# A two-layer attention kernel: head 1's score maxima over three PSUM banks, three of them ahead of the first score step, and two small VectorE operations rewritten as reductions

## The chip, the cores and the metric

The kernel runs on one core of a Trainium2 chip. The metric is device time in microseconds for one launch, which handles all eight images. TensorE does the matrix products and writes them to PSUM (eight banks of 512 fp32 numbers per partition); VectorE (DVE), ScalarE (ACT) and GpSimd (POOL) work on SBUF, the first two on PSUM as well. SyncE (SP) only issues DMAs. Each engine runs its own instructions in order and waits on semaphores for the others.

## The reference

Eight images of 32x32 positions with 384 channels. In short:

```
x = x + conv_attention(group_norm(x, 32 groups))     # 6 heads of 64, 1024 x 1024 scores,
                                                     # plus relative positions rel_h, rel_w
t = tokens(x)
t = t + causal_attention(layer_norm(t))              # 6 heads of 64, causal mask
t = t + gelu(layer_norm(t) @ kron(c_fc_1, c_fc_2).T) @ kron(c_proj_1, c_proj_2).T
attention: qkv = x @ W; softmax(q k^T * scale [+ rel]) v; @ W_out + bias
```

All products keep fp32 accuracy by splitting a number into an fp16 high part and an fp16 low part, and multiplying high x high, high x low and low x high.

## The kernel before, in words

**Order.** Everything is written out by hand, per engine: there is no scheduler. The closures `tensor`, `scalar`, `vector`, `gpsimd` and `sync` inside `build` (L1557 to L1784) issue one image after the other. While one image's feed-forward runs, TensorE already computes the next image's queries and keys between the `up` and `down` products (`after.fill`), then its relative positions (`rel_products`) and the first value tile (`v_products(pe, 0)`).

**An attention** (`class Attention`, L827) works through heads, and each head through G groups of two key tiles for half of the queries: 8 groups per head in the first attention, so 48 steps. A step `i` on TensorE (`tensor`, L1026) is: score products (`score_tiles`, six 128x512 products), one or two small "uses" (`early`), the weighted values of step i - 3 (`weighted_values`, 24 products), more uses (`late`). ScalarE turns scores into exponentials (L1073) and their fp16 high part (L1053); GpSimd, and VectorE in odd steps, make the low part (L1139). A ring of four buffers lies between.

**Maxima.** The softmax of a head subtracts the rows' maxima. For that, TensorE computes the scores another time in coarse form, 16 tiles of 128x512 per head (uses `("max", h, n)`, L941), VectorE takes each tile's maximum over 512 keys into `mxp` (L1097), `combine` (L1132) takes the larger of the two key halves, TensorE transposes the result to a row (use `("row", h)`, L946), VectorE copies it to `rowt` (L1105), and SyncE sends it to one row of `qc` by DMA (`row_in`), from where the last product of a score step (L992) adds it. Head 0's 16 tiles stand in the attention's `prologue`. Head 1's are spread over steps 0 to 4 (four, three, three, three, three), and its row is a late use of step 5. Head h's later tiles are spread in the same way ahead of its row.

**Banks.** Scores use banks 0 to 3 (two per step, in turn). The uses after the first row alternate between banks 4 and 5. Weighted values go to bank 6 for a head's first half and bank 7 for its second. A use waits until VectorE has released (`free`) the last use of its bank. Value tiles `v_products(pe, t)` go to banks 6 and 7 in turn; tile t waits for ScalarE's copies (`v_high`, L815 and L816, semaphore `v32`) of tile t - 2. `rel_high` (ScalarE, L740) and `rel_low` (VectorE, L746) copy the relative positions into the queries, 16 parts per image.

**The feed-forward's end.** VectorE's `low(i)` (`pair_low`, L614) makes the next image's key low parts, one instruction per head of pair i. `o2_out` (L1457) copies the `down` product out of PSUM, and TensorE's `spread` (L1465) waits for it. `eps` (L1264) adds epsilon to the variances, GpSimd's `root` (L1269) raises them to -1/2.

## Time and profile before

| what | value |
|---|---|
| median of 3 runs | 2788.88 us (2784.71 to 2790.33) |
| profiled execution | 2787.91 us, its span 2786.2 us |
| TensorE busy | 2597.0 us, 93% |
| ScalarE busy | 1996.5 us, 72% |
| VectorE busy | 1907.6 us, 68% |
| GpSimd busy | 1680.8 us, 60% |
| granted TensorE clock | 0.989 of full speed (mean) |
| chain of waits that ended last | TensorE 45%, GpSimd 17%, ScalarE 13%, VectorE 13%, issue 11% |

The profile is of one execution. Times in it are microseconds from the span's start. A row of a timeline has start, duration, engine, line, operation, and in brackets the idle time just before it with what ended it. Successive matmuls overlap in it by about 0.16 us, so the duration of a group of them is longer than the time after which the next one is issued. L numbers are lines of this kernel.

### The profile page before, as it was taken

To read this page: it belongs to the slowest core of one execution; us is meant where nothing else is said; L and a number is where in the kernel's file an instruction comes from. 1 tells how busy PE (TensorE), PEld (TensorE's weight loads), DVE (VectorE), ACT (ScalarE), POOL (GpSimd) and SP (SyncE) were. 2 spreads that over 40 slices of the span, in tenths; PEclk is the share of its full clock that TensorE was granted. 3 is DMA by queue.
4 is the path that set the end of the run, shared out by engine and by line. 5 is a ranking of instruction groups with operands and counts; after the bars stand their busy time and mean duration, and the time that the engine had idled before them with its cause. 6 is when DMAs were issued, how large, how long until landed. Compare 5 with 4: busy or idle time off the path is not lost.

```text
span 2786.2 us, 69295 instructions
## 1 busy us (share of the span) xinstructions
PE 2597.0 (93%) x29061; PEld 1540.1 (55%) x29061; DVE 1907.6 (68%) x3554; ACT 1996.5 (72%) x2387; POOL 1680.8 (60%) x1151
## 2 busy tenths in 40 slices
PE   7899999999999999999999999999998999999996
PEld 4465645656456564565645656466564655546563
DVE  8775757667676767757667576675776758677574
ACT  6686867858578595785867867678667777678684
POOL 5474756747567384683756747567465665747464
PEclk8999999999999999999999999999999999999998
DMA  3100012000110002000020000300003000110000
GB/s 110 40 2 2 2 33 72 2 1 2 48 57 2 1 2 76 28 2 1 2 84 21 2 1 2 103 2 2 1 8 97 2 2 2 24 58 2 2 2 24
DMA packets 52278, 64.50 MB, mean 23 GB/s; under 512 B 8672, under 2 KB 46176, under 8 KB 51968
## 3 DMA queue, kind: packets, MB, share of 16 engines
q1 hardware_dynamic: 50208, 59.66, 7.1%
q8 instruction: 231, 3.78, 0.6%
q10 hardware_dynamic: 1760, 0.41, 0.1%
q14 instruction: 79, 0.65, 0.1%
HBM read 30.75 MB, written 12.58 MB: 16 GB/s over the span
## 4 chain that ended last, share of the span: by engine, by line
PE 45%; POOL 17%; ACT 13%; DVE 13%; issue 11%; DMA 0%; SPq 0%; POOLq 0%; ACTq 0%; DVEq 0%
POOL pl L1139 16%; PE ps L571 9%; PE ps L1022 7%; PE ps L802 5%; PE ps L979 4%; PE ps L992 4%; PE ps L941 4%; ACT p L1073 4%; DVE mxp L1097 3%; PE ps L981 3%; ACT ph L1053 3%; DVE stats L1255 2%; DVE x L1251 2%; ACT qa L740 2%; PE ps L1230 2%
## 5 line engine op out<-in xcount | busy, mean ns | idle before, releaser
L1139 POOL TENSOR_TENSOR pl<-p,ph 128x1024 f16<-128x1024 f32 (+2 forms) x672 | 1095.9, 1644 | 366.8 <-ACT ph L1053 360.7
L1097 DVE TENSOR_REDUCE mxp<-ps 128x1 f32<-128x512 f32 (+2 forms) x1344 | 783.6, 626 | 265.4 <-PE ps L941 261.9
L1073 ACT ACTIVATE p<-ps 128x1024 f32<-128x1024 f32 (+1 forms) x672 | 640.3, 953 | 171.9 <-PE ps L992 171.1
L1053 ACT ACTIVATE ph<-p 128x1024 f16<-128x1024 f32 (+1 forms) x672 | 669.3, 996 | 21.4
L1022 PEld LDWEIGHTS ps<-v,ph 128*128 128x128 f16 x9600 | 506.2, 97 | 128.2 <-issue 27.5
L1022 PE MATMUL ps<-v,ph 128*128 128x65 f16 (+1 forms) x9600 | 531.1, 194 | 17.0 <-POOL pl L1139 16.5
L1022 PE MATMUL ps<-v,pl 128*128 128x65 f16 x4800 | 509.2, 192 | 0.0
L1022 PEld LDWEIGHTS ps<-v,pl 128*128 128x128 f16 x4800 | 446.7, 99 | 0.0
L992 PE MATMUL ps<-qc,kc 65*128 65x512 f16 (+3 forms) x1344 | 380.1, 364 | 0.0
L1139 DVE TENSOR_TENSOR pl<-p,ph 128x512 f16<-128x512 f32 (+1 forms) x336 | 243.9, 726 | 183.8 <-ACT ph L1053 182.8
L820 POOL TENSOR_TENSOR v<-o,v 128x384 f16<-128x384 f32 x128 | 115.7, 921 | 309.8 <-ACT o L816 309.3
L979 PE MATMUL ps<-qa,ka 128*128 128x512 f16 x768 | 291.1, 379 | 0.8 <-DVE qb L746 0.8
L981 PE MATMUL ps<-qb,ka 128*128 128x512 f16 x768 | 291.0, 379 | 0.0
L941 PE MATMUL ps<-ka,qa 128*128 128x512 f16 x768 | 256.1, 386 | 32.8 <-DVE mxp L1097 20.5
L992 PEld LDWEIGHTS ps<-qc,kc 65*128 65x128 f16 (+1 forms) x1344 | 123.5, 98 | 126.1 <-issue 1.9
L941 PEld LDWEIGHTS ps<-ka,qa 128*128 128x128 f16 x768 | 74.4, 97 | 170.1 <-DVE mxp L1097 67.2
L979 PE MATMUL ps<-qa,qb 128*128 128x512 f16 (+1 forms) x576 | 162.0, 344 | 2.1 <-ACT p L1073 2.1
L571 PE MATMUL ps<-xin,wqkv_hi 128*128 128x512 f16 x576 | 157.0, 381 | 2.2 <-DVE xin L521 2.2
L941 PE MATMUL ps<-qb,qa 128*128 128x512 f16 (+2 forms) x576 | 154.9, 326 | 0.0
L1126 DVE TENSOR_TENSOR lT<-ps,hT 128x512 f16<-128x512 f32 x96 | 66.4, 691 | 127.4 <-ACT hT L1058 127.4
L815 ACT ACTIVATE v<-ps 128x384 f16<-128x384 f32 x128 | 63.6, 497 | 118.2 <-PE ps L802 117.6
L1443 ACT ACTIVATE p<-ps 128x1024 f32<-128x1024 f32 x96 | 97.6, 1022 | 55.9 <-PE ps L1430 55.3
(197 smaller groups left out, 4664.1 us busy)
## 6 DMA issues: line engine op xcount, KB each, us to landing
xin<-in_x SPq DMA_DIRECT2D x8, 1536.0 KB, 6.8
x<-in_x SPq DMA_DIRECT2D x8, 1536.0 KB, 6.8
out<-x SPq DMA_DIRECT2D x16, 768.0 KB, 3.6
qc<-qa SPq DMA_DIRECT2D x42, 128.0 KB
qa<-qa SPq DMA_DIRECT2D x21, 128.0 KB
qb<-qb SPq DMA_DIRECT2D x21, 128.0 KB, 2.4
qa<-o SPq DMA_DIRECT2D x56, 48.0 KB
qb<-o SPq DMA_DIRECT2D x56, 48.0 KB, 2.0
```

Of the source, the lines that this page charges most:

```text
L571: mm = nc.tensor.matmul(m.ps[:, self.bank[i] + j, :], w[:, k, self.order[i] * P:(self.order[i] + 1) * P], x(k, 4 * j, 4 * j + 4), start=(n ...
L802: mm = nc.tensor.matmul(m.ps[:, 6 + t % 2, 0:C], flat_tile(x(k, t, t + 1)), w[:, k, 2 * C:3 * C], start=(n == 0), stop=(n == len(steps) - 1))
L820: self.nc.gpsimd.tensor_tensor(self.m.v[:, t, :, HD + 1:VW], self.m.o[:, t, :].rearrange("p (h d) -> p h d", d=HD), self.m.v[:, t, :, 0:HD ...
L941: mm = nc.tensor.matmul(m.ps[:, bank, 0:w], m.qa[:, sl, qt * P:(qt + 1) * P], self.ka[:, sl, kh * BANK:kh * BANK + w], start=not diag, sto ...
L979: nc.tensor.matmul(outs[j], self.ka[:, sl, keys[j]], m.qa[:, sl, q], start=True, stop=False)
L981: nc.tensor.matmul(outs[j], self.ka[:, sl, keys[j]], m.qb[:, sl, q], start=False, stop=False)
L992: mm = nc.tensor.matmul(outs[j], m.kc[crows(h), sl, keys[j]], m.qc[crows(h), sl, q], start=False, stop=True)
L1022: mm = nc.tensor.matmul(m.ps[:, 6 + half % 2, c0:c0 + w], e, v, start=(first and n == 0), stop=(g in self.last_of_half and n == len(work) ...
L1053: self.nc.scalar.activation(m.ph[:, i % RING, :, 0:w], m.p32[:, i % RING, :, 0:w], ACT.Copy).then_inc(self.s["hi"], 1)
L1073: nc.scalar.activation(m.p32[:, i % RING, :, 0:w], m.ps[:, 2 * (i % 2):2 * (i % 2) + 2, 0:w], ACT.Exp, scale=SCALE).then_inc(s["exp"], 1)
L1097: nc.vector.reduce_max(m.mxp[:, h % 2, kh, qt:qt + 1], m.ps[:, bank, 0:w], AX.X).then_inc(s["free"], 1)
L1139: engine.tensor_tensor(m.pl[:, i % RING, part, 0:w], m.p32[:, i % RING, part, 0:w], m.ph[:, i % RING, part, 0:w], ALU.subtract).then_inc(s ...
```

## The change

Seven edits, in one file:

1. The combine is a reduction over the two key halves (`reduce_max` on a view of `mxp`) into a tile `top` of its own; tiles that have one key half alone write their maximum to `top` at once. The row matmul reads `top`.
2. The addition of epsilon is a reduction: a third column of `mv` holds 1e-5, and `reduce_sum` adds it to the variance.
3. In the first attention, head 1's first three maximum tiles are issued ahead of score step 0, each followed by a third of the last value tile. The other 13 are spread over steps 0 to 4.
4. These 13 go round banks 4, 5 and 7. The first in bank 7 waits until value tile 7 has been copied out of it; the first weighted values of a head-0 second half wait until the last maximum there has been read.
5. The wait for the low parts of the relative positions (`rel_lows_ready`) moves from behind the last value tile to ahead of these three tiles.
6. ScalarE's copies of value tile 1 of the next image come ahead of the last two `rel_high`.
7. VectorE copies the first `down` product out (`o2_out(0)`) between the two heads of key pair 3.

On TensorE, first attention of the second image, from head 0's row matmul on (L946, in the new kernel L957); L802 (L804) is a value tile's product, L979 to L992 a score step, L941 (L952) a maximum tile. Before:

```order
L946 MATMUL ps<-minus,mxp 8x128
L802 MATMUL ps<-wqkv_hi,xin 128x384
L802 MATMUL ps<-wqkv_lo,xin 128x384
L802 MATMUL ps<-wqkv_hi,xin 128x384 x2
L802 MATMUL ps<-wqkv_lo,xin 128x384
L802 MATMUL ps<-wqkv_hi,xin 128x384 x2
L802 MATMUL ps<-wqkv_lo,xin 128x384
L802 MATMUL ps<-wqkv_hi,xin 128x384
L979 MATMUL ps<-qa,ka 128x512
```

And now:

```order
L957 MATMUL ps<-minus,top 8x128
L952 MATMUL ps<-ka,qa 128x512
L804 MATMUL ps<-wqkv_hi,xin 128x384
L804 MATMUL ps<-wqkv_lo,xin 128x384
L804 MATMUL ps<-wqkv_hi,xin 128x384
L952 MATMUL ps<-ka,qa 128x512
L804 MATMUL ps<-wqkv_hi,xin 128x384
L804 MATMUL ps<-wqkv_lo,xin 128x384
L804 MATMUL ps<-wqkv_hi,xin 128x384
L952 MATMUL ps<-ka,qa 128x512
L804 MATMUL ps<-wqkv_hi,xin 128x384
```

Three maximum tiles moved in between the value products; behind score steps 0 to 4 now stand three, three, two, three and two.

On VectorE, in the first image's feed-forward; L614 (L616) is a key head's low part, L1457 (L1471) the copy of the `down` product, L1480 (L1494) the widening behind the spread. Before:

```order
L614 SCALAR_TENSOR_TENSOR kc<-ps,bqk,ka 64x1024 x2
L1457 COPY pl<-ps 128x512
L1480 TENSOR_TENSOR ph<-ps,cp 128x768
L1480 TENSOR_TENSOR pl<-ps,cp 128x768
L614 SCALAR_TENSOR_TENSOR kc<-ps,bqk,ka 64x1024 x2
```

And now:

```order
L616 SCALAR_TENSOR_TENSOR kc<-ps,bqk,ka 64x1024
L1471 COPY pl<-ps 128x512
L616 SCALAR_TENSOR_TENSOR kc<-ps,bqk,ka 64x1024
L1494 TENSOR_TENSOR ph<-ps,cp 128x768
L1494 TENSOR_TENSOR pl<-ps,cp 128x768
L616 SCALAR_TENSOR_TENSOR kc<-ps,bqk,ka 64x1024 x2
```

The copy stands one key head earlier.

On ScalarE, at the end of the first image; L740 (L742) copies relative positions, L815 and L816 (L817 and L818) a value tile. Before:

```order
L815 ACTIVATE v<-ps 128x6x64
L816 ACTIVATE o<-ps 128x384
L740 ACTIVATE qa<-ps 32x96x8 x4
L815 ACTIVATE v<-ps 128x6x64
L816 ACTIVATE o<-ps 128x384
```

And now:

```order
L817 ACTIVATE v<-ps 128x6x64
L818 ACTIVATE o<-ps 128x384
L742 ACTIVATE qa<-ps 32x96x8 x2
L817 ACTIVATE v<-ps 128x6x64
L818 ACTIVATE o<-ps 128x384
L742 ACTIVATE qa<-ps 32x96x8 x2
```

Value tile 1's two copies stand ahead of the last two copies of relative positions.

The diff:

```diff
--- before.py
+++ after.py
@@ -104,13 +104,14 @@
     m.ph = sb("ph", [P, RING, 2, BANK], F16)
     m.pl = sb("pl", [P, RING, 2, BANK], F16)
     m.stats = sb("stats", [P, NT, 6], F32)
-    m.mv = sb("mv", [P, NT, 2], F32)
+    m.mv = sb("mv", [P, NT, 3], F32)
     m.gstats = sb("gstats", [P, 2, 6], F32)
     m.gmv = sb("gmv", [P, NC_, 2], F32)
     m.small = sb("small", [P, 6, NT], F32)
     m.ln = sb("ln", [P, 3, NT], F32)
     m.rowt = sb("rowt", [NT, P], F16)
     m.mxp = sb("mxp", [P, 2, 2, NT], F32)
+    m.top = sb("top", [P, 2, NT], F32)
     m.minus = sb("minus", [P, P], F32)
     m.rs = sb("rs", [P, 2, 4], F32)
     m.idle = sb("idle", [P, 1], F32)
@@ -291,6 +292,7 @@
             gk = m.group[:, k, :].rearrange("p (g r) -> p g r", r=GC)
             carve(gk, ALU.is_ge, 0.0, GC - 1 - k * P, [[GC, C // GC], [0, GC]], -1, "group_made")
         fill(m.minus_half[:, :], -0.5)
+        fill(m.mv[:, :, 2], 1e-5)
         fill(self.anti, 0.0)
         carve(self.anti, ALU.not_equal, 1.0, -(NREL - 1), [[1, NREL]], 1, "anti_made")
         fill(m.v[:, :, :, HD:HD + 1], 1.0)
@@ -851,18 +853,21 @@
 
         self.prologue = [("max", 0, n) for n in range(self.NTL)]
         steps = [[] for _ in range(self.N)]
+        self.beside_row = []
         if self.causal:
             self.prologue += [("max", 1, n) for n in range(self.NTL)]
             self.prologue.insert(self.NTL + ROW_AFTER, ("row", 0))
             ends = [0, 0] + [h * G - ROW_LEAD for h in range(2, NH)]
         else:
             ends = [0] + [h * G - ROW_LEAD for h in range(1, NH)]
-            steps[0].append(("row", 0))
+            self.beside_row = [("max", 1, n) for n in range(NC_)]
+            steps[0] += [("row", 0)] + self.beside_row
         for h in range(1, NH):
             begin, end = ends[h - 1], ends[h]
             if end > begin:
-                for n in range(self.NTL):
-                    steps[begin + n * (end - begin) // self.NTL].append(("max", h, n))
+                ahead = len(self.beside_row) if h == 1 else 0
+                for n in range(ahead, self.NTL):
+                    steps[begin + (n - ahead) * (end - begin) // (self.NTL - ahead)].append(("max", h, n))
             steps[end].append(("row", h))
         for c in range(NC_ - 1):
             for hf in range(2):
@@ -890,6 +895,10 @@
         ahead = (4, 5, 0, 1, 2, 3) if self.causal else (0, 1)
         first = len(self.prologue) + (not self.causal)
         self.banks = [ahead[r % len(ahead)] if r < first else 4 + r % 2 for r in range(len(self.index))]
+        self.beside_values = [] if self.causal else [self.index[("max", 1, n)] for n in range(NC_, self.NTL)]
+        for n in range(NC_ if not self.causal else self.NTL, self.NTL):
+            self.banks[self.index[("max", 1, n)]] = (4, 5, 7)[n % 3]
+        self.beside_values = [r for r in self.beside_values if self.banks[r] == 7]
         self.last_use = [max((q for q in range(r) if self.banks[q] == self.banks[r]), default=None) for r in range(len(self.index))]
         self.scores_after = [max((q for q, bank in enumerate(self.banks) if bank in (2 * i, 2 * i + 1)), default=None) for i in range(2)]
 
@@ -916,7 +925,7 @@
         return self.prologue[self.beside_v[t]:self.beside_v[t + 1]]
 
     def early(self, i):
-        return [u for u in self.uses_at[i][:2] if u[0] == "max" or u == ("row", 0)]
+        return [u for u in self.uses_at[i][:2 + (len(self.beside_row) if i == 0 else 0)] if u[0] == "max" or u == ("row", 0)]
 
     def late(self, i):
         return self.uses_at[i][len(self.early(i)):]
@@ -935,6 +944,8 @@
             _, h, n = u
             qt, kh, w = self.tiles[n]
             sl = slot(h)
+            if self.beside_values and r == self.beside_values[0]:
+                pe.wait_ge(self.proj.s["v32"], self.proj.s.at("v32", NT))
             diag = self.causal and (qt + 1) * P - kh * BANK <= BANK
             if diag:
                 nc.tensor.matmul(m.ps[:, bank, w - P:w], m.identb[:, :], m.mask_qk[:, :], start=True, stop=False, skip_group_check=True)
@@ -943,7 +954,7 @@
         elif u[0] == "row":
             _, h = u
             pe.wait_ge(s["combined"], s.at("combined", h + 1))
-            mm = nc.tensor.matmul(m.ps[0:NT, bank, 0:P], m.mxp[:, h % 2, 0, :], m.minus[:, :], start=True, stop=True, skip_group_check=True)
+            mm = nc.tensor.matmul(m.ps[0:NT, bank, 0:P], m.top[:, h % 2, :], m.minus[:, :], start=True, stop=True, skip_group_check=True)
         elif u[0] == "unit":
             if u[1] == 0:
                 pe.wait_ge(self.next_in, 16 * (self.norm_.s.image + 1))
@@ -1003,6 +1014,8 @@
             pe.wait_ge(self.proj.s["v_lo"], self.proj.s.at("v_lo", NT))
         if first and half >= 2:
             pe.wait_ge(s["out"], s.at("out", half - 1))
+        if first and half == 1 and self.beside_values:
+            pe.wait_ge(s["free"], s.at("free", self.beside_values[-1] + 1))
         self.wait_hi(pe, i)
         self.wait_lo(pe, i)
         work = []
@@ -1031,7 +1044,7 @@
                     last_values()
                 self.score_tiles(pe, i)
                 for u in self.early(i):
-                    if u != ("row", 0):
+                    if u != ("row", 0) and u not in self.beside_row:
                         self.use(pe, u)
             else:
                 between(i - self.N)
@@ -1094,7 +1107,8 @@
             _, h, n = u
             qt, kh, w = self.tiles[n]
             dve.wait_ge(s["use"], s.at("use", r + 1))
-            nc.vector.reduce_max(m.mxp[:, h % 2, kh, qt:qt + 1], m.ps[:, bank, 0:w], AX.X).then_inc(s["free"], 1)
+            to = m.mxp[:, h % 2, kh, qt:qt + 1] if qt >= self.both.start else m.top[:, h % 2, qt:qt + 1]
+            nc.vector.reduce_max(to, m.ps[:, bank, 0:w], AX.X).then_inc(s["free"], 1)
             if n == self.NTL - 1:
                 self.combine(dve, h)
         elif u[0] == "row":
@@ -1129,7 +1143,7 @@
 
         nc, m, s, both = self.nc, self.m, self.s, self.both
         dve.wait_ge(s["free"], s.at("free", self.index[("max", h, self.NTL - 1)] + 1))
-        nc.vector.tensor_tensor(m.mxp[:, h % 2, 0, both], m.mxp[:, h % 2, 0, both], m.mxp[:, h % 2, 1, both], ALU.max).then_inc(s["combined"], 1)
+        nc.vector.reduce_max(m.top[:, h % 2, both], m.mxp[:, h % 2, :, both].rearrange("p k t -> p t k"), AX.X).then_inc(s["combined"], 1)
 
     def low_part(self, eng, engine, i, sem, part):
         m, w = self.m, self.cols(i)
@@ -1256,12 +1270,12 @@
 
     def aggregate(self, dve, t):
         dve.wait_ge(self.s["stats"], self.s.at("stats", t + 1))
-        self.nc.vector.bn_aggr(self.m.mv[:, t, :], self.m.stats[:, t, :]).then_inc(self.s["mv"], 1)
+        self.nc.vector.bn_aggr(self.m.mv[:, t, 0:2], self.m.stats[:, t, :]).then_inc(self.s["mv"], 1)
 
     def eps(self, dve, hf):
         dve.wait_ge(self.s["mv"], self.s.at("mv", 4 * (hf + 1)))
         t = slice(4 * hf, 4 * hf + 4)
-        self.nc.vector.tensor_scalar(self.m.ln[:, 0, t], self.m.mv[:, t, 1], 1e-5, None, ALU.add).then_inc(self.s["eps"], 1)
+        self.nc.vector.reduce_sum(self.m.ln[:, 0, t], self.m.mv[:, t, 1:3], AX.X).then_inc(self.s["eps"], 1)
 
     def root(self, pool, hf):
         t = slice(4 * hf, 4 * hf + 4)
@@ -1586,8 +1600,10 @@
 
             def beside_row():
 
-                qkv0.v_products(pe, NT - 1)
                 qkv0.rel_lows_ready(pe)
+                for c in range(NC_):
+                    attn0.use(pe, attn0.beside_row[c])
+                    qkv0.v_products(pe, NT - 1, [c])
             attn0.tensor(pe, proj0.between(pe), beside_row)
             proj0.rest(pe)
             ln.tensor(pe, 0)
@@ -1647,7 +1663,7 @@
         def scalar(act, w, before):
             qkv0, attn0, ln, qkv1, attn1, ff = w.qkv0, w.attn0, w.ln, w.qkv1, w.attn1, w.ff
             for t in range(NT):
-                if t > 0 or not before:
+                if t > 1 or not before:
                     qkv0.v_high(act, t)
                 for n in w.with_v[t]:
                     for r in range(4 * n, 4 * n + 4):
@@ -1684,7 +1700,10 @@
                 for r in range(8, 12):
                     w.next.qkv0.rel_high(act, r)
                 w.next.qkv0.v_high(act, 0)
-                for r in range(12, 16):
+                for r in range(12, 14):
+                    w.next.qkv0.rel_high(act, r)
+                w.next.qkv0.v_high(act, 1)
+                for r in range(14, 16):
                     w.next.qkv0.rel_high(act, r)
 
         def vector(dve, w, before):
@@ -1720,8 +1739,9 @@
             low(2)
             if w.next:
                 w.next.qkv0.rel_rows_low(dve, 0)
-            low(3)
+            low(3, (0,))
             ff.o2_out(dve, 0)
+            low(3, (1,))
             ff.widen(dve, 0)
             ff.widen(dve, 1)
             low(4)
```

## Rows read from the trace of the kernel before

**Rows 1.** The page's first section: busy time, share of the span, instructions.
```profile
PE 2597.0 (93%) x29061; PEld 1540.1 (55%) x29061; DVE 1907.6 (68%) x3554; ACT 1996.5 (72%) x2387; POOL 1680.8 (60%) x1151
```

**Rows 2.** Timeline of TensorE, 777 to 798 us: start, duration, instruction, [idle before].
```profile
777.73 0.39 PE L946 MATMUL ps<-minus,mxp 128*8 128x128 f32 x2
...
779.52 0.38 PE L979 MATMUL ps<-qa,ka 128*128 128x512 f16 x1
...
780.82 0.60 PE L941 MATMUL ps<-ka,qa 128*128 128x512 f16 x2
781.99 0.39 PE L941 MATMUL ps<-ka,qa 128*128 128x512 f16 x1 [0.57 <-DVE mxp L1097]
...
789.98 0.23 PE L1022 MATMUL ps<-v,ph 128*128 128x65 f16 x2
...
790.72 0.38 PE L941 MATMUL ps<-ka,qa 128*128 128x512 f16 x1
...
797.44 0.39 PE L946 MATMUL ps<-minus,mxp 128*8 128x128 f32 x2 [1.11 <-DVE mxp L1097]
```

**Rows 3.** Timeline of VectorE, the same stretch.
```profile
781.24 2.48 DVE L1097 TENSOR_REDUCE mxp<-ps 128x1 f32<-128x512 f32 x4 [2.80 <-PE ps L941]
...
795.18 1.60 DVE L1132 TENSOR_TENSOR mxp<-mxp 128x8 f32<-128x8 f32 x1
```

**Rows 4.** Timeline of GpSimd, the same stretch.
```profile
794.62 2.13 POOL L1139 TENSOR_TENSOR pl<-p,ph 128x1024 f16<-128x1024 f32 x1 [1.24 <-ACT ph L1053]
```

**Rows 5.** Timeline of ScalarE, the same stretch.
```profile
781.02 1.02 ACT L1073 ACTIVATE p<-ps 128x1024 f32<-128x1024 f32 x1 [0.42 <-PE ps L992]
782.07 1.06 ACT L1053 ACTIVATE ph<-p 128x1024 f16<-128x1024 f32 x1
```

**Rows 6.** Timeline of all engines, 743 to 746 us, before the spread.
```profile
743.60 1.29 DVE L614 SCALAR_TENSOR_TENSOR kc<-ps,bqk,ka 64x1024 f16<-64x1024 f32 x1 [0.77 <-ACT ka L593]
...
743.87 0.81 PE L571 MATMUL ps<-xin,wqkv_hi 128*128 128x512 f16 x3
...
744.92 0.69 DVE L1457 COPY pl<-ps 128x512 f32<-128x512 f32 x1
...
745.67 1.08 PE L1465 MATMUL ps<-spread,pl 128*128 128x32 f32 x8 [0.99 <-DVE pl L1457]
```

**Rows 7.** Timelines of ScalarE, TensorE and VectorE, 759 to 777 us.
```profile
759.08 3.28 ACT L740 ACTIVATE qa<-ps 32x768 f16<-32x768 f32 x4
...
763.14 0.51 ACT L815 ACTIVATE v<-ps 128x384 f16<-128x384 f32 x1
...
763.31 0.34 PE L802 MATMUL ps<-wqkv_hi,xin 128*128 128x384 f16 x1 [1.36 <-ACT o L816]
...
766.66 10.42 DVE L1097 TENSOR_REDUCE mxp<-ps 128x1 f32<-128x512 f32 x16 [0.52 <-PE ps L941]
```

**Rows 8.** Timelines of GpSimd and VectorE, 709 to 715; durations (ns) of all L1132.
```profile
709.23 3.10 POOL L1363 TENSOR_TENSOR o<-x,cf 128x384 f32<-128x384 f32 x3 [5.58 <-DVE x L1251]
...
711.76 0.53 DVE L1368 TENSOR_REDUCE ph<-o 128x32 f32<-128x384 f32 x1
...
714.39 0.98 DVE L1264 TENSOR_SCALAR ln<-mv 128x4 f32<-128x4 f32 x1
...
L1132 DVE TENSOR_TENSOR mxp<-mxp x96: 161/166/1606, 95.0 to 2715.7; 128x8 f32<-128x8 f32 x48, 128x4 f32<-128x4 f32 x48
```

**Rows 9.** Timeline of TensorE in the first image, score step 0.
```profile
99.73 0.39 PE L979 MATMUL ps<-qa,ka 128*128 128x512 f16 x1 [0.77 <-DVE qb L746]
```

**Rows 10.** Timeline of TensorE, head 2's row matmul.
```profile
867.91 0.39 PE L946 MATMUL ps<-minus,mxp 128*8 128x128 f32 x2 [0.28 <-DVE mxp L1097]
```

**Rows 11.** Timeline of TensorE, third and last image's feed-forward.
```profile
727.84 0.61 PE L1430 MATMUL ps<-ph,c 96*128 96x512 f16 x2 [0.19 <-DVE ph L1418]
...
2752.11 1.03 PE L1405 MATMUL ps<-ident,ph 128*32 128x128 f32 x4 [6.06 <-DVE x L1251]
```

**Rows 12.** Stretches: us, TensorE busy (instructions), granted clock, DMA share, GB/s.
```profile
80.00:100.00 20.00, 15.14 (x43) 0.66 0.01 1
```

## The prediction

> **What bounds the kernel now.** I read the page first. TensorE is busy 93% of the span [rows 1]; the next, ScalarE, has 72%. So a change pays where TensorE stands still, or where something late holds it, and nowhere else. Next I read TensorE's timeline through one image (the third of eight; the images follow each other every 340 us and look alike) and wrote down every place where it is idle and who releases it. There are few, and four are what this change is about:
>
> - Between the row matmul of head 0 (777.73) and that of head 1 (797.44) of the first attention TensorE stands still five times: 0.57, 0.2 (the tile behind it), twice 0.57 again (785.27 and 787.96) and 1.11 us, each time released by VectorE's maxima, L1097 [rows 2]. The first four are the wait for a PSUM bank: tiles of maxima alternate between two banks, TensorE issues one in 0.22 us, VectorE takes 0.62 us for one (four in 2.48) [rows 3]. The fifth is the wait for the combined maxima: VectorE's combine at 795.18 took 1.60 us for 128x8 numbers [rows 3], and ended with GpSimd's subtraction, which ran from 794.62 to 796.75 [rows 4].
> - At the first spread of the feed-forward TensorE waits 0.99 us for VectorE's copy at 744.92, which stands behind the last half of a key pair's low part (743.60) [rows 6].
> - At the image's start it waits 1.36 us for ScalarE's second value tile, 763.14, which stands behind four copies that began at 759.08 [rows 7].
> - In the feed-forward's input, VectorE's addition of epsilon, 128x4 numbers, took 0.98 us [rows 8], once per image.
>
> **Part 1: between the two rows (three banks, three tiles ahead, a combine that is a reduction).** The work that TensorE does between the two row matmuls stays the same; it is only put in another order. Packed without waits it is: row matmul and last value tile 1.79 us (777.73 to 779.52); six score steps at 1.30 (779.52 to 780.82); 16 tiles of head 1 and two of head 2 at 0.216; three steps of weighted values at 0.74 (789.98 to 790.72) [rows 2]. 1.79 + 7.80 + 3.89 + 2.22 = 15.70 us, against 19.71 now: 4.0 us are there to be won per image.
>
> Do they come? I walked the new order with the old durations, from the row matmul as 0. The three tiles issue at 0.32, 1.03 and 1.73, where VectorE was idle before (the idle stretch ended at 781.24); the third wants the bank of the first, free at 1.5. Score step 0 starts at 2.43. Its correction product needs the row back by DMA, which was there at 2.65 before (779.52 + 4 x 0.216 = 780.38, with no idle time), and is wanted at 3.3 now. Tiles 3, 4, 5 issue at 3.7 to 4.2, the last into the third bank, which needs the value copy of ScalarE (about 3.5). Step 1 starts at 4.4, and its third tile finds its bank free at 6.17 when TensorE comes at 6.11. After that no bank is waited for: a step with three tiles takes TensorE 1.95 us and VectorE 1.86, one with two less. ScalarE needs 1.02 + 1.06 us a step [rows 5] and has its scores two steps ahead of need; GpSimd's 2.13 us subtractions end about 2 us before the weighted values want them. The sixteenth maximum ends at 13.8, the combine at 14.0, and row 1 is issued at about 15.75. The added wait of the second half's weighted values for the third bank falls at step 7, while the last maximum in that bank is read in step 4: behind that wait nothing queues. What is left over: VectorE's own subtraction at 14.0 has two SBUF inputs, as the slow combine had, and may wait for a GpSimd one; two maxima queue behind it, and row 1 takes the bank of one of them. I take 0.2 us for it. So 3.8 per image, between 2.9 (only the two-bank waits go, and one of 1.11 stays) and 4.0.
>
> In the first image TensorE waits until 99.73 for VectorE's low parts of the relative positions [rows 9]. That wait is now ahead of the last value tile, which used to hide 1.47 us of it. So 3.8 - 1.4 = 2.4 there. In the other images these low parts end before 766.66 [rows 7], eleven us before they are wanted, and the moved wait costs nothing. Sum of part 1: 7 x 3.8 + 2.4 = 29.0 us.
>
> **The combine as a reduction** matters by itself at head 2's row: 0.28 us idle at 867.91 in seven images [rows 10]. I count 0.4 each, as an idle time leaves out 0.16 us of the overlap of two matmuls: 2.8 us. The trace has no reduction of 16 numbers; the shortest combine took 0.16 and half of them no more than 0.17 [rows 8], and a maximum over 512 takes 0.62, so it lies between, nearest to the small one by its size. Whether a reduction out of SBUF waits for GpSimd: VectorE's sum at 711.76 (L1368, 384 numbers) took 0.53 us in the middle of GpSimd's third multiplication, which ended at 712.33 [rows 8]: it didn't. Bounds for the wait 0 and 1.4 us.
>
> The trace's combine ends when GpSimd's subtraction ends. The Trainium skill says why (SBUF — State Buffer, Who interferes with whom): a VectorE instruction with two SBUF inputs, or one in a 2-port mode such as tensor_scalar, waits for the whole of a GpSimd instruction that reads SBUF, while tensor_reduce never does on this chip. By that rule both rewritten operations become free, and the sum at 711.76 agrees (0.53 us beside a busy GpSimd). If the rule failed, the sum would be the second rival's.
>
> **Part 2: the spread.** VectorE is idle for 0.77 us ahead of the second key half at 743.60 [rows 6]. The copy (0.69) fits in just that gap, since TensorE has long gone on from the products that it reads to others of the next image; so the key half starts at 743.6 as before, and TensorE goes on at 744.52 instead of 745.67 (the three products at 743.87 issue every 0.216) [rows 6]: 1.15 us, seven images. Everything up to the image's end hangs on TensorE and ScalarE in turn, and moves with it.
>
> **Part 3: value tile 1 ahead of two copies.** TensorE's third tile (t=3) then needs no wait; the next is bound by the third value copy, which ends where it did, since ScalarE does the same work: 759.08 + 3.28 + 2 x 0.9 = 764.2, and TensorE's own time for that tile was 763.31 + 9 x 0.163 = 764.78. That gives 0.5. It can't be more, since VectorE's four low parts before the first maximum at 766.66 [rows 7] have to be done: with part 2's 1.15 they are free at 765.0, where the first maximum comes too. From there VectorE sets the pace for ten us, before as after. Parts 2 and 3: 1.65 x 7 = 11.6 us; bounds 0.5 (only what part 3 gives) and 2.2 per image.
>
> **Part 4: epsilon.** 0.98 becomes 0.17 or so. In the last image, which has no next one to fill TensorE (6.06 idle), all 0.8 count. In the seven others only the second x2 low part gets earlier; the first `up` product waits 0.19 us for it [rows 11], and could win 0.35: 0.8 + 2.4 = 3.2 us, bounds 0 and 6.4. The small fill added at the start is less than 0.3 us behind the weights' loading.
>
> **Sum.** 29.0 + 2.8 + 11.6 + 3.2 = 46.6 us. The profiled execution took 2787.9 us (its span 2786.2), so 2741.3; the median shown is 1.0 above it. I predict 2742.
>
> **The rivals.**
>
> - *Part of the early gain is given back within the attention.* The five steps become 1.95 to 2.7 us long and a ring of four buffers lies behind them; if GpSimd or the exponentials became the pace, TensorE would wait at the weighted values instead. For: GpSimd has the second share of the chain of waits, 17%. Against: ScalarE has 2.08 of work [rows 5] per step of 2.47 (1.30 + two tiles + 0.74). Half of part 1 lost: 2742 + 14 = 2756.
> - *The rewritten operations wait as the old ones did*, so that the change doesn't do what it says there. In head 1 the combine would start at 13.8 and end by 15.4, still before row 1 is due, so only head 2's 2.8 and epsilon's 3.2 are lost: 2748.
> - *The starts don't add up.* The move of 1.15 us meets a DMA or VectorE, and only half of parts 2 and 3 arrives: 2748 too.
> - *Slower: TensorE's clock.* From 80 to 100 us it was granted 0.66 of full speed, so some 14 of the 20 us at the 1.2 GHz level, with TensorE idle for a quarter of them [rows 12]. The new timing moves where idle moments fall. At 1.2 GHz each us of packed work costs one more. The place would be the start of each image's first attention; it decides when more than 46.6 / 8 = 5.8 us of packed work per image fall to that level. A stretch of 14 us at that level in each image (as in the first one) costs 7 us, and gives 2742 + 56 = 2798. Against: the change takes idle time away and adds it only in the first image. Short falls that cost 1 us in some images are in the range.
>
> **How the numbers follow.** Forecast (all four parts, within 5 us) 0.61; half of part 1 given back 0.12; reductions wait 0.05; starts don't add up 0.12; up to 10 us more than forecast 0.04; slower by the clock 0.03; everything absorbed by waits that I don't see 0.03. Range 2733 to 2757: it takes in all rivals but the clock and total absorption. What a measurement of this kernel can tell from no change is 0.2%, 5.6 us; only the last two cases end above 2783: faster 0.94, same 0.03, slower 0.03.
>
> **What the changed profile should show.** Row 0 to row 1 in 15.7 to 16.1 us instead of 19.7, no wait of TensorE for L1097's successor there, or at most 0.1; the combine at 0.2 us everywhere; epsilon at 0.2; no wait at the first spread; at the value tiles one wait of about 0.9 us at t=4 instead of 1.36 at t=3; in the first image a wait of 2.4 us behind row 0. The distance between images shrinks from 340.4 to about 334.2. I am wrong if the weighted values wait for GpSimd in steps 3 to 8, if TensorE's clock leaves 1.00 in those stretches, or if the time from the first maximum to row 0 (766.66 to 777.73) changes.

## The result, and the profile after

The changed kernel takes 2744.77 us (median of 4 runs, 2741.56 to 2747.08), the kernel before 2789.61 us beside it (4 runs, 2784.71 to 2791.53). The ratio is 0.9841, 95% interval 0.9823 to 0.9859: 1.6% faster. The forecast was 2742 us.

The profiled execution of the changed kernel took 2746.77 us, with a span of 2745.0; before it was 2786.2. These 41.2 us are what the two traces have to explain. The page's first section answers to [rows 1]: TensorE is busy for the same time, in a shorter span.

```profile
PE 2597.4 (95%) x29061; PEld 1551.0 (57%) x29061; DVE 1896.2 (69%) x3554; ACT 1995.0 (73%) x2387; POOL 1682.1 (61%) x1152
```

Timeline of TensorE in the third image's first attention, from head 0's row (L957) to head 1's; it answers to [rows 2].

```profile
770.41 0.39 PE L957 MATMUL ps<-minus,top 128*8 128x128 f32 x2
770.72 0.39 PE L952 MATMUL ps<-ka,qa 128*128 128x512 f16 x1
...
771.44 0.38 PE L952 MATMUL ps<-ka,qa 128*128 128x512 f16 x1
...
772.14 0.38 PE L952 MATMUL ps<-ka,qa 128*128 128x512 f16 x1
...
772.85 0.38 PE L990 MATMUL ps<-qa,ka 128*128 128x512 f16 x1
...
786.18 0.38 PE L957 MATMUL ps<-minus,top 128*8 128x128 f32 x2
```

Row to row takes 15.77 us instead of 19.71, and not one row in between has an idle time ahead of it. The early tiles issue 0.31, 1.03 and 1.73 us behind the row. TensorE's waits for GpSimd's low parts, in front of the weighted values, are the same in the whole of both profiles (us in total, times, longest; before, then after):

```profile
PE ps L1022 <- POOL pl L1139: 16.5, 40, 0.8
PE ps L1035 <- POOL pl L1153: 16.5, 40, 0.8
```

So the attention behind the new order gives nothing back.

VectorE at the end of the stretch from row to row [rows 3], and at head 4's row, 70 us further on:

```profile
784.19 0.17 DVE L1146 TENSOR_REDUCE top<-mxp 128x8 f32<-128x16 f32 x1
784.28 1.00 DVE L1153 TENSOR_TENSOR pl<-p,ph 128x512 f16<-128x512 f32 x1
...
854.32 0.17 DVE L1146 TENSOR_REDUCE top<-mxp 128x8 f32<-128x16 f32 x1
854.41 1.51 DVE L1153 TENSOR_TENSOR pl<-p,ph 128x512 f16<-128x512 f32 x1
855.84 1.28 DVE L1111 TENSOR_REDUCE mxp<-ps 128x1 f32<-128x512 f32 x2
```

GpSimd, in answer to [rows 4], was in the middle of this at head 4's combine:

```profile
854.21 1.16 POOL L493 TENSOR_TENSOR xin<-hT,xin 128x512 f16<-128x512 f32 x1
```

Before, VectorE stood like this ahead of head 4's row [rows 10]:

```profile
865.58 1.08 DVE L1132 TENSOR_TENSOR mxp<-mxp 128x8 f32<-128x8 f32 x1
866.58 0.68 DVE L1139 TENSOR_TENSOR pl<-p,ph 128x512 f16<-128x512 f32 x1
```

The combine is free of the wait now; the subtraction behind it has it instead. From the combine's start to the subtraction's end are 1.68 us before and 1.60 after. Head 4's row still waits (TensorE, answering to [rows 10]):

```profile
856.58 0.39 PE L957 MATMUL ps<-minus,top 128*8 128x128 f32 x2 [0.20 <-DVE mxp L1111]
```

The change of image, VectorE and TensorE, in answer to [rows 6] and [rows 7], and the epsilon reduction, in answer to [rows 8]:

```profile
709.27 0.16 DVE L1278 TENSOR_REDUCE ln<-mv 128x4 f32<-128x8 f32 x1
...
737.42 0.69 DVE L1471 COPY pl<-ps 128x512 f32<-128x512 f32 x1
738.15 1.29 DVE L616 SCALAR_TENSOR_TENSOR kc<-ps,bqk,ka 64x1024 f16<-64x1024 f32 x1
...
739.03 0.97 PE L1479 MATMUL ps<-spread,pl 128*128 128x32 f32 x8
...
757.45 0.34 PE L804 MATMUL ps<-wqkv_hi,xin 128*128 128x384 f16 x1 [0.78 <-ACT o L818]
...
759.43 10.34 DVE L1111 TENSOR_REDUCE mxp<-ps 128x1 f32<-128x512 f32 x16
```

The copy now stands ahead of the key half, the spread has no idle time ahead of it, and one wait of 0.78 us at a value tile is left of 1.36.

To see where the whole span went, I cut both timelines of TensorE at the same instructions (first maximum, the rows of heads 0, 1 and 5, the layer norm, and so on) and subtracted the pieces, image by image, before minus after. The column "forecast" has the prediction's terms.

| piece | forecast, us | measured, us |
|---|---|---|
| row of head 0 to row of head 1, images 1 to 7 | 26.6 | 27.5 (3.93 or 3.94 each) |
| the same, first image (image 0) | 2.4 | -0.3 |
| the "head 2" row wait | 2.8 | 0.5, and 0.6 given back before the layer norm |
| to the spread, and to the first maximum | 11.6 | 12.2 (7 x 1.16 + 4.1) |
| feed-forward's entry (epsilon) | 3.2 | 3.3 (7 x 0.35 + 0.8) |
| layer norm and second attention's input | 0 | -3.4 |
| the last spread, and the rest | 0 | 2.0 |
| sum | 46.6 | 41.2 |

Of the last 2.0 us, 0.9 lie ahead of the last image's spread and 0.8 between the two spreads of the seven others.

The layer norm's loss is one of the clock. Stretches of before and of after (us, busy of PE, PEld, DVE, ACT, POOL, granted clock, DMA share, GB/s), both from image 1's layer norm, aligned to its first transposition (587.2 before, 581.2 after):

```profile
586.00:590.00 4.00, 2.30 (x14) 1.38 (x12) 2.88 (x10) 3.13 (x6) 0.97 (x1) 1.00 0.00 0
590.00:594.00 4.00, 3.29 (x20) 1.79 (x19) 1.96 (x4) 3.58 (x7) 0.58 (x2) 1.00 0.02 4
```

```profile
580.00:584.00 4.00, 2.30 (x11) 1.38 (x9) 2.90 (x10) 3.01 (x5) 0.95 (x1) 0.89 0.00 0
584.00:588.00 4.00, 4.00 (x18) 2.19 (x16) 2.15 (x4) 3.49 (x7) 0.06 (x1) 0.68 0.01 4
```

The work is the same and so is TensorE's idle time at the stage's start (0.89 us and three times 0.27, in both kernels). Its first row, before and after:

```profile
587.21 0.33 PE L1316 MATMUL ps<-ident,o 128*128 128x128 f32 x1 [0.89 <-ACT o L1279]
581.24 0.33 PE L1330 MATMUL ps<-ident,o 128*128 128x128 f32 x1 [0.89 <-ACT o L1293]
```

From the layer norm to the next row takes 41.11 us at the full 2.4 GHz, and 41.9 to 42.1 us where part of it ran at 1.2 GHz. That happens in 2 of 8 images of the profile before and in 6 of 8 after.

In the first image the clock is involved as well (TensorE, after; it answers to [rows 9]):

```profile
96.86 0.60 PE L957 MATMUL ps<-minus,top 128*8 128x128 f32 x2
99.79 0.61 PE L952 MATMUL ps<-ka,qa 128*128 128x512 f16 x1 [2.33 <-DVE qb L748]
100.19 0.53 PE L804 MATMUL ps<-wqkv_hi,xin 128*128 128x384 f16 x1
...
104.77 0.63 PE L990 MATMUL ps<-qa,ka 128*128 128x512 f16 x1
105.20 0.42 PE L992 MATMUL ps<-qb,ka 128*128 128x512 f16 x1
```

The wait of 2.33 us is the forecast one. But behind it a product issues every 0.32 us instead of 0.16, so at 1.2 GHz, up to 105 us; before, the clock had reached 2.4 GHz by then, as this stretch of the kernel before shows (granted clock 0.89, and 1.00 in the next 4 us).

```profile
96.00:100.00 4.00, 3.23 (x17) 1.32 (x16) 2.18 (x3) 1.74 (x4) 0.94 (x2) 0.89 0.00 1
```

### The profile page after: what moved, and what is told of

The parts are those of the page before. It is cut to its first block, busy times and chain, and to the rows that moved or that the text cites. A ratio compares the mean times of both kernels' runs of the same rounds, so it can differ in the third digit from the quotient of the medians.

```text
span 2745.0 us, 69295 instructions
## 1 busy us (share of the span) xinstructions
PE 2597.4 (95%) x29061; PEld 1551.0 (57%) x29061; DVE 1896.2 (69%) x3554; ACT 1995.0 (73%) x2387; POOL 1682.1 (61%) x1152
## 4 chain that ended last, share of the span: by engine, by line
PE 56%; POOL 17%; DVE 10%; issue 9%; ACT 8%; DMA 0%; SPq 0%; POOLq 0%; ACTq 0%; DVEq 0%
POOL pl L1153 16%; PE ps L573 12%; PE ps L1035 9%; PE ps L990 5%; PE ps L1003 5%; PE ps L952 5%; PE ps L804 4%; PE ps L992 4%; PE ps L1244 4%; DVE mxp L1111 3%; DVE qb L748 2%; ACT ph L1066 2%; PE ps L1444 2%; ACT p L1086 2%; PE ps L1465 1%
## 5 line engine op out<-in xcount | busy, mean ns | idle before, releaser
L1111 DVE TENSOR_REDUCE mxp<-ps 128x1 f32<-128x512 f32 (+2 forms) x1152 | 700.2, 651 | 196.1 <-PE ps L952 190.5
L1035 PEld LDWEIGHTS ps<-v,ph 128*128 128x128 f16 x9600 | 506.2, 97 | 131.0 <-issue 27.5
L1035 PE MATMUL ps<-v,ph 128*128 128x65 f16 (+1 forms) x9600 | 531.2, 194 | 17.0 <-POOL pl L1153 16.5
L1153 DVE TENSOR_TENSOR pl<-p,ph 128x512 f16<-128x512 f32 (+1 forms) x336 | 257.1, 765 | 183.8 <-ACT ph L1066 182.8
L992 PE MATMUL ps<-qb,ka 128*128 128x512 f16 x768 | 291.7, 380 | 0.0
L952 PE MATMUL ps<-ka,qa 128*128 128x512 f16 x768 | 252.3, 385 | 20.0 <-DVE mxp L1111 5.5
L952 PEld LDWEIGHTS ps<-ka,qa 128*128 128x128 f16 x768 | 74.5, 97 | 145.8 <-DVE mxp L1111 34.5
L952 PE MATMUL ps<-qb,qa 128*128 128x512 f16 (+2 forms) x576 | 154.9, 326 | 0.0
L817 ACT ACTIVATE v<-ps 128x384 f16<-128x384 f32 x128 | 63.5, 496 | 123.9 <-PE ps L804 123.2
L1220 POOL TENSOR_TENSOR x<-x,bo 128x384 f32<-128x384 f32 (+1 forms) x72 | 117.5, 1632 | 32.7 <-ACT o L1293 32.7
```

What stands on the lines that cost most here:

```text
L952: mm = nc.tensor.matmul(m.ps[:, bank, 0:w], m.qa[:, sl, qt * P:(qt + 1) * P], self.ka[:, sl, kh * BANK:kh * BANK + w], start=not diag, sto ...
L992: nc.tensor.matmul(outs[j], self.ka[:, sl, keys[j]], m.qb[:, sl, q], start=False, stop=False)
L1035: mm = nc.tensor.matmul(m.ps[:, 6 + half % 2, c0:c0 + w], e, v, start=(first and n == 0), stop=(g in self.last_of_half and n == len(work) ...
L1111: nc.vector.reduce_max(to, m.ps[:, bank, 0:w], AX.X).then_inc(s["free"], 1)
L1153: engine.tensor_tensor(m.pl[:, i % RING, part, 0:w], m.p32[:, i % RING, part, 0:w], m.ph[:, i % RING, part, 0:w], ALU.subtract).then_inc(s ...
L1220: self.nc.gpsimd.tensor_tensor(m.x[:, t, :], m.x[:, t, :], m.bo[self.layer][:, :].unsqueeze(1).broadcast_to([P, t.stop - t.start, C]), ALU ...
```

## The experiments

Twelve variants, in three groups; within a group all ran on one chip, beside the kernel before (its median 2788.33, 2787.93 and 2788.11 us). Two of them have one execution only. "Row piece" is the stretch from head 0's row to head 1's.

**The new order and banks without the reductions and without the changes at the image's boundary.** Against the changed kernel:

```diff
-            nc.vector.reduce_max(to, m.ps[:, bank, 0:w], AX.X)
+            nc.vector.reduce_max(m.mxp[:, h % 2, kh, qt:qt + 1], m.ps[:, bank, 0:w], AX.X)
...
-        nc.vector.reduce_max(m.top[:, h % 2, both], ...)
+        nc.vector.tensor_tensor(m.mxp[:, h % 2, 0, both], ..., ALU.max)
... (epsilon, value columns and spread as before)
```

> The new order of head 0's row and head 1's largest scores with the three banks alone: the combine of two columns, the eps addition, and the orders of the value columns and of the spread are those of before. Theory: the stretch from head 0's row to head 1's gives its 3.94 us in each of images 1 to 7 and loses 0.30 us in the first, as between the two profiles, since the old two-input combine, though it waits over 1 us for its input port, ends before head 1's row is due: 7 x 3.9 - 0.3 = 27 us, and the layer norm's short falls of the TensorE clock, which that saving moved, stay: about 2763 us beside 2789.6. Rival: the combine's wait shows at row 1 now that the maxima come late; then it costs up to 1.3 us in each of 8 images and the time is about 2773 us.

Measured: 2760.37 us (ratio 0.9901, 0.9886 to 0.9915). The row piece gives 3.93 or 3.94 us in each of images 1 to 7: the same as the whole change. In the first image it gives 0.9 us where the expectation had a loss of 0.3; what differs there is the clock (below, at the first image in the old order). The rival fell: the old combine costs the row nothing once the order is new.

**The combine's reduction alone, in the kernel before.**

```diff
+    m.top = sb("top", [P, 2, NT], F32)
...
-        nc.vector.tensor_tensor(m.mxp[:, h % 2, 0, both], ..., ALU.max)
+        nc.vector.reduce_max(m.top[:, h % 2, both], m.mxp[:, h % 2, :, both]..., AX.X)
```

> Before, with the combine of a head's two halves as one reduction over two columns into an array of its own, and nothing else. Theory: at row 1 the 1.1 to 1.3 us wait of the combine for the second input ends, and the row comes that much sooner in each of 8 images: 8 to 10 us, about 2780 us. Rival: the wait for the port moves to the next two-input instruction on VectorE in front of what TensorE waits for, as it did between the two profiles at the row of head 4 (combine 0.17, then the subtraction 1.51 us); the time stays at 2788 to 2790 us.

Measured: 2780.31 us (0.9972, 0.9960 to 0.9984). The row piece gives 1.17 to 1.19 us in each of 8 images. So the reduction is worth 8 us by itself, and the new order 28, by the medians. Both work on the same stretch, and the next variant shows that they do not add up. VectorE at row 1 there:

```profile
791.00 0.68 DVE L1141 TENSOR_TENSOR pl<-p,ph 128x512 f16<-128x512 f32 x1
...
792.32 0.17 DVE L1134 TENSOR_REDUCE top<-mxp 128x8 f32<-128x16 f32 x1
```

In this order the subtraction comes ahead of the combine, in a moment when GpSimd is between two instructions (one ends at 790.53 us, the next starts at 791.77), so nothing takes the wait over.

**The whole change with the old combine.**

```diff
-        nc.vector.reduce_max(m.top[:, h % 2, both], ...)
+        nc.vector.tensor_tensor(m.mxp[:, h % 2, 0, both], ..., ALU.max)
```

> After, with the old combine of two columns in place of the reduction. Theory: alone in the kernel before the reduction brought 8 us, but the new order has the row's inputs early enough that the two-input combine's wait of about 1 us only takes the place of the wait that the subtraction behind it has now: within 2 us of after, about 2746 us. Rival: the two savings add up, and without the reduction the time is 2752 us.

Measured: 2746.25 us (0.9850, 0.9835 to 0.9865), the same as the changed kernel within what runs tell. The row piece of images 1 to 7 differs by 0.01 us at most. VectorE at row 1, then TensorE's row:

```profile
781.19 0.57 DVE L1145 TENSOR_TENSOR mxp<-mxp 128x8 f32<-128x8 f32 x1
781.69 0.68 DVE L1152 TENSOR_TENSOR pl<-p,ph 128x512 f16<-128x512 f32 x1
...
783.18 0.39 PE L957 MATMUL ps<-minus,mxp 128*8 128x128 f32 x2
```

Combine and subtraction together take 1.18 us here and 1.09 in the changed kernel: one wait for the port, put down to the one instruction or to the other. The combine ends 1.4 us before the row issues, which has no idle time.

**Two banks instead of three.**

```diff
-            self.banks[self.index[("max", 1, n)]] = (4, 5, 7)[n % 3]
+            self.banks[self.index[("max", 1, n)]] = (4, 5)[(n + 1) % 2]
```

> After, with head 1's largest scores in the two banks 4 and 5 in turn and none in the bank of the weighted values. Theory: the four early tiles beside the row come at the pace of the reductions again, two in flight instead of three, and the TensorE waits for a free bank some 1 to 2 us longer in each image: 2753 to 2760 us beside 2744.8. Rival: the order does the work and the third bank is worth nothing: 2745 us.

Measured: 2757.76 us (0.9889, 0.9875 to 0.9904). The row piece is 1.56 us longer in each of images 1 to 7, by two waits of the old kind:

```profile
778.86 0.39 PE L952 MATMUL ps<-ka,qa 128*128 128x512 f16 x1 [0.57 <-DVE mxp L1111]
...
781.55 0.39 PE L952 MATMUL ps<-ka,qa 128*128 128x512 f16 x1 [0.57 <-DVE mxp L1111]
```

Twice 0.57 idle plus the 0.16 us of overlap that an idle time leaves out is 1.46 of the 1.56. (The expectation said four early tiles; there are three.)

**Three banks, but no tile beside the row.**

```diff
-            self.beside_row = [("max", 1, n) for n in range(NC_)]
+            self.beside_row = []
...
+                qkv0.v_products(pe, NT - 1)
```

> After, with no tile of head 1 beside the row: the 16 tiles spread over the steps as before, but over the three banks. Theory: the early tiles beside the row fill most of the idle behind head 0's row, and without them 2 to 3 us of the 3.94 us of each image are lost: 2760 to 2766 us. Rival: the third bank carries the gain; 2750 us or less.

Measured: 2752.30 us (0.9868, 0.9852 to 0.9885). Only 0.87 us per image is lost, not 2 to 3: the rival, that the third bank carries most of the gain, is nearer. TensorE waits 0.35 and 0.17 us for L1111 (and twice 0.16 of overlap):

```profile
775.91 0.39 PE L952 MATMUL ps<-ka,qa 128*128 128x512 f16 x1 [0.35 <-DVE mxp L1111]
...
787.25 0.39 PE L952 MATMUL ps<-ka,qa 128*128 128x512 f16 x1 [0.17 <-DVE mxp L1111]
```

So with the reduction in place the row piece goes 1.18 (reduction alone), 2.38 (with early tiles), 3.07 (with the third bank instead), 3.94 (with both): the bank carries more than the tiles.

**The orders at the image's boundary, and the spread's alone, in the kernel before.**

```diff
-            low(3)
+            low(3, (0,))
             ff.o2_out(dve, 0)
+            low(3, (1,))
... (only in the first of the two:)
-                if t > 0 or not before:
+                if t > 1 or not before:
                     qkv0.v_high(act, t)
...
+                w.next.qkv0.v_high(act, 1)
```

> Before, with the order of the value columns on ScalarE and of the spread on VectorE at the change of image alone. Theory: these two carry the boundary's 1.16 + 0.57 + 0.1 = 1.83 us in each of 7 changes of image: 12.8 us, about 2777 us. Rival: part of that gain was there only because the row's stretch had changed too; then half of it or less, 2783 us and more.

> Before, with the order of the spread on VectorE alone, the value columns as before. Theory: 1.15 us at each of 7 changes of image in the stretch to the spread's first matmuls, and none of the 0.57 us in front of the first largest scores, which belongs to the value columns on ScalarE: 8 us in the profile. Rival: the two are one path, and this edit alone gives both or neither.

Measured: both 2774.93 us (0.9956, 0.9939 to 0.9972); the spread alone 2778.94 us (one execution). The piece to the spread gives 1.14 to 1.16 us with both and 1.13 to 1.15 with the spread alone, in each of seven images. The piece to the first maximum gives 4.1 us over images 1 to 7 with both, and with the spread alone nothing (-0.1 over the same images). Two paths, which add up, as forecast.

**Epsilon alone, in the kernel before.**

```diff
-        self.nc.vector.tensor_scalar(self.m.ln[:, 0, t], self.m.mv[:, t, 1], 1e-5, None, ALU.add)
+        self.nc.vector.reduce_sum(self.m.ln[:, 0, t], self.m.mv[:, t, 1:3], AX.X)
```

> Before, with the eps addition as a reduction alone. Theory: the feed-forward's entry gives 0.35 us in each of images 1 to 7 and 0.8 us in the last, 3.3 us in the profile, and no other stretch changes but for the clock's falls. Rival: the gain needs the other edits; 0.

Measured: 2786.46 us (one execution). The feed-forward's entry gives 0.34 to 0.36 us in seven images and 0.79 in the last, 3.2 us. The execution's span is only 1.5 us shorter: the layer norm's stretch lost 1.2 us to the clock's falls (3 images instead of 2), and another fall, at the end of the fifth image (granted clock 0.89 and 0.68 from 1778 to 1786 us), cost 0.6 more.

**The first image in the old order.** All seven others are as in the changed kernel.

```diff
+                if not before:
+                    qkv0.v_products(pe, NT - 1)
                 qkv0.rel_lows_ready(pe)
                 for c in range(NC_):
                     attn0.use(pe, attn0.beside_row[c])
-                    qkv0.v_products(pe, NT - 1, [c])
+                    if before:
+                        qkv0.v_products(pe, NT - 1, [c])
```

> After, and in the first image alone the last value tile's products (7 of before) stand ahead of the wait for the low parts again, with the three early tiles behind them. Theory: the 2.33 us idle at 97.5 us of the profile of after goes, the TensorE keeps its full clock there, and the 2.3 to 3 us that the first image lost come back: about 2742 us. Rival: the idle moves behind the products and the clock falls all the same; 2745 us.

Measured: 2743.76 us (0.9844, 0.9829 to 0.9858), no difference that the runs tell. In the profile the first image's row piece is 3.62 us shorter than after: the wait is 0.76 us instead of 2.33, and the clock stays up; but the layer norm's stretch now has the clock's fall in all 8 images. And the profile of the variant with the old combine has the same 2.33 us of idle time in the first image as the changed kernel, and there the clock had risen already. Its row piece is 2.38 us shorter than before: the forecast's 2.4. Stretches of TensorE, first of after, then of that variant:

```profile
92.00:96.00 4.00, 3.76 (x10) 1.44 (x11) 2.74 (x5) 0.00 (x0) 0.00 (x0) 0.50 0.00 0
96.00:100.00 4.00, 1.67 (x6) 0.38 (x5) 2.18 (x3) 0.87 (x2) 0.88 (x1) 0.50 0.00 1
100.00:104.00 4.00, 4.00 (x13) 1.74 (x12) 2.08 (x3) 0.00 (x0) 0.00 (x0) 0.50 0.00 0
```

```profile
92.00:96.00 4.00, 4.00 (x13) 1.49 (x12) 1.71 (x4) 0.17 (x1) 0.00 (x0) 0.50 0.00 0
96.00:100.00 4.00, 1.67 (x10) 0.79 (x9) 3.09 (x5) 0.70 (x2) 0.89 (x1) 0.91 0.00 1
100.00:104.00 4.00, 4.00 (x21) 1.86 (x20) 2.68 (x5) 2.57 (x4) 0.89 (x1) 1.00 0.45 106
```

So the loss in the first image needs a low clock behind the wait, and the order alone does not settle that. But it makes it likely. Five profiles have the wait of 2.33 us; the clock granted from 100 to 104 us is 0.50 in the changed kernel and with two banks, 0.57 with no tile beside the row, 0.75 with the reorder alone, and 1.00 with the old combine alone. With no tile beside the row and with the reorder alone the clock had risen ahead of the wait, and fell again behind it. The nine other profiles wait 0.77 us at most there, and all have 1.00.

**Filling the layer norm's idle time.** Four matmuls whose results nothing reads, on top of the variant before.

```diff
             proj0.rest(pe)
+            for _ in range(4):
+                nc.tensor.matmul(m.ps[:, 4, :], m.wo_hi[0][:, 0, 0:P], m.wqkv_hi[1][:, 0, 0:BANK], start=True, stop=True)
             ln.tensor(pe, 0)
```

> As the variant with the first image's order, and four more matmuls of 512 columns into a bank that is free then, ahead of the layer norm's TensorE work in each image, whose results nothing reads. Theory: they fill an idle behind the last projection, the clock does not fall in the layer norm's stretch, and up to 0.9 us in each of 6 images comes back: 2736 to 2739 us. Rival: the idle that the clock answers to is a later one, or the four matmuls (4 x 0.22 us) delay what follows: 2742 to 2749 us.

Measured: 2740.56 us (0.9831, 0.9816 to 0.9846), 3.2 us below the variant without them, though above the 2736 to 2739 us of the theory. In images 0 to 6 the layer norm's stretch is 41.13 us and its granted clock 1.00; the eighth has a fall (0.70 and 0.87 below) and takes 42.54. The four matmuls stand in the 0.89 us of idle time and cost nothing.

```profile
576.00:580.00 4.00, 3.14 (x17) 1.60 (x15) 2.81 (x12) 3.38 (x6) 1.01 (x1) 1.00 0.02 4
580.00:584.00 4.00, 3.30 (x20) 2.01 (x21) 1.77 (x3) 3.58 (x7) 0.76 (x1) 1.00 0.00 0
2572.00:2576.00 4.00, 3.33 (x15) 1.55 (x14) 1.96 (x4) 3.92 (x7) 0.73 (x1) 0.70 0.00 2
2576.00:2580.00 4.00, 4.00 (x23) 2.48 (x22) 1.51 (x3) 1.61 (x4) 3.83 (x1) 0.87 0.00 0
```

**Three more, in the next idle time of the same stage.**

```diff
             ln.tensor(pe, 0)
+            for _ in range(3):
+                nc.tensor.matmul(m.ps[:, 3, :], m.wo_hi[0][:, 0, 0:P], m.wqkv_hi[1][:, 0, 0:BANK], start=True, stop=True)
```

> The variant with four filling matmuls before the layer norm's transposes, and three more behind their first half, into the 0.67 us that the TensorE waits there for the low part. Theory: the clock's fall in the last image's layer norm, the one that was left, goes too: 1.4 us less, about 2739 us. Rival: the three matmuls (0.65 us) stand beside an idle that was their whole cover and cost up to 0.1 us in each of 8 images, or the last fall has another reason: 2740.5 to 2742 us.

Measured: 2737.53 us (2736.74 to 2739.43; ratio 0.9818, 0.9803 to 0.9833), the lowest median of this study; each of its four runs is below each run of the changed kernel. It was measured on another chip than the variant with four matmuls, and the intervals of the two ratios overlap, so the medians do not tell the two apart. All eight layer norms run at 1.00 and take 41.11 us; the last one gives 1.43 us. The same place in the last image:

```profile
2571.00:2575.00 4.00, 3.93 (x24) 2.01 (x22) 1.96 (x4) 3.89 (x7) 0.60 (x1) 1.00 0.01 2
2575.00:2579.00 4.00, 4.00 (x23) 2.34 (x24) 1.89 (x3) 1.57 (x3) 3.97 (x1) 1.00 0.00 0
```

**The four filling matmuls in the kernel before** (the same edit).

> Before, with the four filling matmuls ahead of the layer norm's transposes and nothing else. Theory: the layer norm's falls of the clock are none of the change's doing; they go here too, two of 8 images in the profile of before: 1 to 2.5 us less, about 2786.5 us, and the granted clock is 1.00 in each image's layer norm. Rival: with so few falls the four matmuls bring nothing or cost up to 0.2 us in each image: 2788 to 2790 us.

TensorE where the idle time was (L1594 is the four matmuls):

```profile
585.74 1.03 PE L1594 MATMUL ps<-wqkv_hi,wo_hi 128*128 128x512 f16 x4
586.79 0.33 PE L1316 MATMUL ps<-ident,o 128*128 128x128 f32 x1
```

Measured: 2789.12 us over 10 runs (2784.08 to 2791.43; ratio 1.0001, 0.9992 to 1.0011). The profile agrees with the theory (all eight layer norms at 1.00, 1.9 us gained there, its span 2784.0), but the median shows no gain: the rival's number. That profile has a fall elsewhere, at the end of the fifth image (0.90 and 0.68 in the two stretches of 4 us from 1776 us), which takes 0.8 us back; three other profiles have one in that place too (epsilon alone, reorder alone, old combine). The other nine runs left no trace, but each has its mean granted clock on record, and the time goes with it: four runs at 0.989 or 0.990 have spans of 2782.4 to 2784.9 us, six at 0.987 or 0.988 have 2787.1 to 2789.7. So the spread from run to run goes with the clock; in which stages it fell in the slower runs stays open, and with it why the median shows no gain.

## Why the prediction was right, and where it was not

*Part 1, the row piece.* Forecast 3.8 of a possible 4.0, measured 3.93 or 3.94 in each of seven images. The walk through the new order holds to a tenth of a microsecond (third early tile at 1.73, row 1 at 15.77 against 15.75). The 0.2 us kept back for the subtraction was not needed. The runs add what the walk didn't show: the third bank is worth 1.56 and the early tiles 0.87, each with the rest in place, and the reduction nothing.

*First image.* Forecast +2.4, measured -0.3. The wait was forecast (2.4, measured 2.33). The step that failed is that the work behind it was priced at 2.4 GHz: in the profiled execution it ran at 1.2 GHz for 5 us more. Where the clock was up, in one of the five profiles with this wait, the term came to 2.38. The rival of the clock, which was given 3 in 100 at 56 us, is real, but small: 2.7 us here and 3.4 in the layer norms, a place that it didn't name.

*The combine at "head 2's row".* This term of 2.8 us failed twice. 867.91 is head 4's row, and not head 2's as [rows 10] and the prediction call it; head 2's had no wait. And the step "the combine is free, so the row comes 0.4 earlier" left out that the wait for the port goes to the next instruction with two SBUF inputs, which stands right behind the combine and ahead of two maxima, one of which holds the row's bank. The row comes 0.06 to 0.09 us earlier in seven images, the difference between 1.68 and 1.60, and that is given back before the layer norm. The prediction saw this mechanism in head 1, where it cost nothing, and not in head 4, where it cost the whole term.

VectorE's two reductions themselves took 0.17 and 0.16 us wherever they stand. By the Trainium skill (SBUF — State Buffer, Who interferes with whom) a tensor_reduce never contends with GpSimd on this chip, and an instruction with two SBUF inputs does contend with a GpSimd instruction that reads SBUF. The traces agree with both halves, the second at 1.00 and 1.51 us for the subtraction against 0.68 without a wait.

*Parts 2 and 3.* Forecast 1.65 per change of image (1.15 + 0.5), measured 1.16 + 0.58, and the two single edits show them separate and additive. *Part 4.* Forecast 3.2, measured 3.3 in the whole change and 3.2 alone. Both choices between bounds far apart (0.5 to 2.2, 0 to 6.4) rested on one row that TensorE waits at, and held.

*Not forecast.* The layer norm's stretch lost 3.4 us, in a place that the change does not touch. The prediction counted "short falls that cost 1 us in some images" into the range; there were four more of them than before, at 0.8 or 0.9 each. The last image's spread gained 0.9, since the clock came back 11.4 us behind the feed-forward's first transposition instead of 14.0. That gain is luck: the filled kernel before, which changes nothing there, has it too (0.95), and the spread's order alone does not (-0.1).

*The rivals.* "Part of the early gain is given back" fell: TensorE's waits for GpSimd are 16.5 us in both profiles. The rewritten operations did not wait, yet the 2.8 us that this rival put at risk were lost by another way. The starts added up. Of the signs, the distance from image to image came to 334.58 us (334.2 forecast), and from the first maximum to row 0 TensorE takes 11.48 us as before; the clock did leave 1.00 behind the first image's row.

The forecast of 2742 us is 2.8 below the median. Between the profiles the sum is 5.4 off: the terms that came out larger (+0.9 in the row piece, +0.6 at the boundary, +0.1 with epsilon, +2.0 in the rest) make up for less than half of those that failed (-2.7, -2.9 and -3.4). Half of the 5.4 falls away in the medians: the profile of after lies 2.0 us above its own, and the forecast had 0.7 added for that of before. So it is in part luck that the total is this close.

How often the clock falls in the layer norm, by profile, in 8 images: before 2, reduction alone 4, boundary orders 3 and 2 (spread alone, both), epsilon 3; after 6, old combine 4, reorder alone 4, two banks 3, no early tiles 5, first image's order 8. That is 14 of 40 with the old row piece and 30 of 48 with the new one, one profile each: a hint that the change makes falls more frequent, no proof. The mean granted clock, which is on record for runs without a profile too, points the same way: 0.984 to 0.987 in the four runs of the changed kernel, 0.986 to 0.989 in 29 of the kernel before. That the falls hang on the idle time is shown by the filled kernels (0 of 8 twice, 1 of 8 once); that it isn't enough for one is shown by image 7 of after, which has nearly the same idle times (0.90 and three times 0.27 us) and no fall. Over the images 1 to 7 of after the rows of head 0 follow each other by 334.58 us each time, and the clock falls at the same place in images 1 to 6; before, the distance was 339.8 to 340.9. What decides in which images it falls stays open. The Trainium skill (TensorE: Matmul & The Clock Gate, Part 1: The HAM clock gate) says that the moment at which the clock rises varies from run to run. No two traces here are of one kernel, but the changed kernel and the one with the old combine do the same on TensorE up to there, and they agree with it: 0.50 against 0.91 granted from 96 to 100 us.
